# One order changed inside a tick: TensorE's search products first, ScalarE's relu of the search first

## The reference, cut to what matters

```python
# layer 0: two 3x3 convolutions with leaky relu, then a mamba block over L = 4096 tokens
h = exp(d_t * A) * h + (d_t * u_t) * b_t        # scan, 128 channels x 16 states
y = sum_n h * c_t                               # then gate with silu(z) and project
# layer 1
energy_c = xc @ xc.T ; out_c = softmax(energy_c) @ x          # 64 x 64
energy_s = q.T @ k ; attn_s = softmax(energy_s, -1)           # 4096 x 4096
out_s = v @ attn_s.T
out = x + w_bn @ concat(out_c, out_s)
```

## Time and profile before

| | |
|---|---|
| median of 3 runs | 9451.27 us (9447.06 to 9454.93) |
| profiled execution, its own time | 9445.67 us |
| its span, first to last instruction | 9443.9 us |
| mean granted TensorE clock | 0.964 |
| busy share PE, DVE, ACT, POOL | 88%, 79%, 67%, 34% |

### The profile page before, as it was taken

The page is one execution under the profiler, slowest core; times in us unless marked ns, Lnnn a source line. Parts: engine busy times, 40 slices in busy tenths (PEclk is TensorE's granted clock), DMA queues, the critical chain, the costliest instruction groups (busy, mean ns, idle before and its releaser), DMA issues. The chain is left out here.

```text
span 9443.9 us, 135784 instructions
## 1 busy us (share of the span) xinstructions
PE 8334.9 (88%) x38977; PEld 2213.4 (23%) x39622; DVE 7490.6 (79%) x11112; ACT 6298.8 (67%) x12445; POOL 3166.4 (34%) x2315
## 2 busy tenths in 40 slices
PE   7884369998999999998999999998999999989999
PEld 2221112222222222222222222222222222222222
DVE  1114998888898888888898988888898989888832
ACT  1112457777777777777777777777777777777754
POOL 0002543333333333333333333333333333333300
PEclk9997669999999999999999999999999999999999
DMA  5556786766676776766676766766676767667610
GB/s 90 82 85 139 202 204 167 187 171 170 171 178 172 178 183 169 182 173 170 171 181 170 177 174 173 182 173 171 172 178 172 185 171 177 174 166 178 153 27 6
DMA packets 805909, 1511.55 MB, mean 160 GB/s; under 512 B 349800, under 2 KB 383280, under 8 KB 805168
## 3 DMA queue, kind: packets, MB, share of 16 engines
q1 hardware_dynamic: 802096, 1502.63, 65.1%
q10 hardware_dynamic: 3072, 0.40, 0.0%
HBM read 1309.36 MB, written 176.16 MB: 157 GB/s over the span
## 5 line engine op out<-in xcount | busy, mean ns | idle before, releaser
L1208 POOL TENSOR_TENSOR hst<-hst,cbc 128x512 f32<-128x512 f32 x2048 | 2807.6, 1371 | 4892.0 <-ACT carry L965 4289.1
L954 ACT ACTIVATE pr<-bank 128x512 f32<-128x512 f32 x4096 | 2225.7, 597 | 976.4 <-PE bank L836 874.8
L1102 DVE TENSOR_TENSOR_SCAN hst<-dA,carry,bank 128x512 f32<-128x512 f32 x1792 | 2294.0, 1280 | 64.0
L845 PE MATMUL bank<-pr,vt 128*64 128x512 f32 x8192 | 2218.3, 620 | 0.0
L1044 DVE CUSTOM_DVE_ANT_0 gains<-bank,gains 128x512 f32<-128x512 f32 x2048 | 1406.6, 687 | 825.7 <-ACT gains L900 799.6
L1092 DVE TENSOR_TENSOR bank<-lanes,bbc 128x512 f32<-128x512 f32 x2048 | 1707.5, 834 | 79.9 <-DMA lanes<-spread_d 35.2
L782 PE MATMUL bank<-s1kx,s1q 128*128 128x512 bf16 x4096 | 1348.4, 389 | 439.2 <-DVE mxp L1044 398.9
L960 ACT ACTIVATE dA<-lanes,small 128x512 f32<-128x512 f32 x2048 | 1489.2, 727 | 237.4 <-DMA lanes<-spread_d 141.5
L836 PE MATMUL bank<-t2q,t2k 128*128 128x512 bf16 x4096 | 1563.2, 382 | 90.0 <-issue 34.8
L834 PE MATMUL bank<-s1q,s1k 128*128 128x512 bf16 x3451 | 1330.8, 386 | 138.7 <-ACT pr L954 96.9
L900 ACT ACTIVATE gains<-bank 128x512 f32<-128x512 f32 x2048 | 1234.4, 603 | 231.9 <-PE bank L782 226.8
(11 more groups left out here) (110 smaller groups left out, 6369.8 us busy)
## 6 DMA issues: line engine op xcount, KB each, us to landing
lanes<-spread_d SPq DMA_DIRECT2D x2048, 512.0 KB, 5.1
seqt<-seq_d SPq DMA_DIRECT2D x256, 128.0 KB, 4.6
spread_d<-dsp SPq DMA_DIRECT2D x128, 256.0 KB, 2.0
spread_d<-usp SPq DMA_DIRECT2D x128, 256.0 KB, 2.0
bbc<-bc_d SPq DMA_DIRECT2D x128, 256.0 KB, 3.4
cbc<-bc_d SPq DMA_DIRECT2D x128, 256.0 KB, 3.9
xpad<-in_x SPq DMA_DIRECT2D x64, 256.0 KB, 6.4
ypad<-ypad SPq DMA_DIRECT2D x128, 128.0 KB, 2.8
```

The source lines that it names most:

```text
L845: mm = nc.tensor.matmul(ACC[CH * h:CH * (h + 1), :], vt[:, t, :], pr[:, T % PRING, h, :], start=t == 0, stop=t == KT - 1)
L954: nc.scalar.activation(pr[:, T % PRING, h, :], bank_of(("S", T, h))[:], ACT.Exp).then_inc(S["p_full"], 1)
L1102: nc.vector.tensor_tensor_scan(hst[:, T % HRING, :], dA[:, T % 2, :], DBU[:], carry[:, g:g + 1] if sl % CHUNKS else 0.0, ALU.mult, ALU.add ...
L1208: nc.gpsimd.tensor_tensor(h, h, cbc[:, (T - 1) // GROUPS % 2, :], ALU.mult).then_inc(S["hc_in"], 1)
```

## The change

TensorE's tick begins with the search pair; the scores, PV, SUM or Y, and the small products follow. So six bf16 matmuls stand together, and all fp32 products behind them. ScalarE's tick begins with the relu of the search; exp, exp, dA, carry and the rest follow. The ring's order changes with the plan. VectorE's, GpSimd's and SyncE's orders stay as they are, and so does every instruction; only places and the semaphore values that follow from them differ.

```diff
@@ plan
         uses, plan = self.small_uses(T), []
+        near = 2 if self.searches(T) else 0
+        plan += uses[0:near]
         if self.attends(T):
             plan += [("S", T, 0), ("S", T, 1)]
         if self.attends(T - 1):
             plan.append(("PV", T - 1))
-        plan += uses[0:2]
...
-        return plan + uses[2:]
+        return plan + uses[near:]
@@ ScalarE's loop over ticks
                         sl, r = T // GROUPS, T % GROUPS
+                        near = 2 if sched.searches(T) else 0
+                        for e in sched.small_uses(T)[0:near]:
+                            small_use(e)
                         if sched.attends(T):
...
-                        for e in sched.small_uses(T):
+                        for e in sched.small_uses(T)[near:]:
                             small_use(e)
```

## The result

| | before | changed |
|---|---|---|
| median | 9447.06 us (9440.51 to 9454.93, 5 runs) | 9595.04 us (9589.41 to 9598.87, 5 runs) |
| ratio to before | 1 | 1.0157, interval 1.0143 to 1.0171 |
| span of the profiled execution | 9443.9 us | 9596.5 us |
| mean granted TensorE clock | 0.964 | 0.956 |

The change costs 148 us. The forecast was 83 us faster; the time lies in the stated range, on the other side. In the experiments they shift by a few more.

A forecast was written before the change was run, and what follows sets the result against it. Neither VectorE nor TensorE alone bounds; 0.43 us a tick is lost handing over. Relu -1.44, handover +1.3, GpSimd and dt -0.5, times 120 chunks, give -77, with the tail -83: 9368 us; 8 in 10 for 9200 to 9600.

The forecast's parts named there:

- the handover: At r = 10 to 11, scores and PV stand behind max, costing 1.72 us; savings of 0.4 leave net +1.3 per chunk.
- So it is hidden: ScalarE's exp and dA, delayed by max, take 2.6 us from the reduction; the scan wants dA after at least 3.3.
- the pin: max waits for the previous tick's reduction to leave its bank, so scores and PV behind it cannot run ahead.
- The relu at r = 1, -1.44: ScalarE's relu moved first is out before VectorE's tap ends, removing its whole 1.44 us idle per chunk.
- my own rival: Much faster: slack pays for the handover and relu waits vanish everywhere (452 waits, 408 us); about 9170 us, chance 0.15.
- The pair's 0.44: On TensorE, the search pair's distance falls to 0.44 us in all ticks, from 0.53 where narrow fp32 follows.
- GpSimd and VectorE, -0.5 with dt in it: In VectorE's stretch: L1156 -0.85, dt at most +1.0, DBUs and L1150 -0.9 to +2; taken as -0.5 us per chunk.
- The rival on the port: Slower by GpSimd's port: four of nine VectorE-stretch ticks pay 0.67 - 0.12 us each at DBU; 9596 us, chance 0.17.
- The dt wait: The dt product stands 1.97 us later behind the pair; at r = 7 VectorE gets it at most 1.0 us late.
- Slower by the pin: Handover costs 1.5, dt's full 1.0 shows, TensorE can't run ahead: +1.1 per chunk, about 9580 us, chance 0.18.
- Its last part, the clock: Longer single waits might lower TensorE's granted clock once every second chunk, about 1.7 us each, another 100 us.
- the wait at L1139: Sign of being wrong: VectorE waiting over 1 us at L1139, where the late dt product shows.

The follow-up runs named there:

- e5: Changed kernel with only max moved, to directly behind the four score matmuls; dif and the early relu stay: 9370.25 us, 0.9926 of the kernel before.
- e6: e4 plus one added TensorE wait, ahead of the scores, for the reduction of the tick before: 9731.83 us, 1.0306 of the kernel before.
- e11: e5 with ScalarE's order of before, the relu behind carry: 10001.47 us, 1.0583 of the kernel before.
- e7: Kernel before with GpSimd's multiplication by C cut to 16 of 512 columns, leaving out part of the computation: 9124.3 us, 0.9662 of the kernel before.
- e8: Changed kernel with GpSimd's multiplication by C cut to 16 of 512 columns, leaving out part of the computation: 9430.55 us, 0.9987 of the kernel before.
- e3: Changed kernel with small products moved ahead of PV and SUM or Y, except at r = 0: 9580.16 us, 1.0141 of the kernel before.
- e4: Changed kernel with only max moved, behind the scores and PV; dif and relu stay first: 9392.64 us, 0.9943 of the kernel before.
- e10: e5 with ScalarE's carry copy moved ahead of both exps: 9474.98 us, 1.003 of the kernel before.

## Why the prediction was wrong

The step that failed is the handover, priced as **"+1.3"** per chunk for one place, r = 10 to 11. The mechanism was named rightly; its size and its extent were not. TensorE's wait for the reduction in the matmul rows grew from 272.4 us in 1413 ticks to 503.5 us in 1383, that is from 3.1 to 5.8 us in 16 ticks, +2.7, and from three waits in 16 ticks to five (276 and 431 in all). The forecast also had only `max` held, where `dif` is held in 129 of them. Behind it come waits of VectorE that the sum had only for dt: all its waits but the one for the relu rose by 6.0 us in 16 ticks. The sentence on ScalarE, "So it is hidden", held for what it names: the scan waits 22.0 us in 5700 for dA. It is what ScalarE makes of late products that VectorE waits for. e5 and e6 show that the pin decides: moving `max` takes 225 us off, putting its wait back in front of the scores costs 339 us.

- *The relu at r = 1, -1.44.* The direction was right, the term too small: the relu's wait fell from 408 us in 1413 ticks to 60 in 1383, from 4.6 to 0.7 us in 16 ticks. At the very place that was priced it came true and was taken back: in a tick r = 1 of the changed kernel the reduction follows the tap with no wait, but the tap waits 2.27 us for L990, where the earlier trace rows had 0.76.

```profile
8803.78 0.75 DVE L1122 SCALAR_TENSOR_TENSOR cacc<-xin,small,cacc 128x512 f32<-128x512 f32 x1 [2.27 <-ACT cacc L990]
8804.56 0.69 DVE L1048 CUSTOM_DVE_ANT_0 gains<-bank,gains 128x512 f32<-128x512 f32 x1
```

Over the whole stretch this wait rose from 58.1 to 98.7 us; the forecast had let it stay. e11 puts the whole lever at 631 us with e5's order. That the forecast counted one place and the waits showed 452 of them stood in my own rival.
- *The pair's 0.44.* Right: 8781.70 to 8782.15 in the changed kernel's timeline.
- *GpSimd and VectorE, -0.5 with dt in it.* Its two halves must be read apart. L1156 fell from 1258 to 422 ns (-0.84 priced as -0.85), and DBU rose from 824 to 875 ns (+0.8 in 16 ticks), so these two cancel. L1150, which the sum named without a sign, fell from 1132 to 692 ns. Others it did not have: the split behind L1156 (L1161, now L1165) rose from 968 to 1406 ns, and each of the three taps of a chunk fell from 897 to 787. VectorE's work in all fell by 0.6. The rival on the port fell with that, and with e7 and e8; that its number, 9596, is the nearest of all is luck. The Trainium skill (SBUF — State Buffer, Who interferes with whom) calls the port pair that VectorE shares with GpSimd an exclusive lock. The stretched means agree with it. The dt wait was bounded by 1.0 and measured 124.0 / 87 = 1.4 us.
- *Left out.* res, en, turn, PV's copy and Y at its reader L1088: 61 + 69 + 39 + 39 + 31 = 239 us of VectorE's waits in 5700, against 17 before, and 66 us more before the scan. I had moved every small product by 1.97 us and followed only dt. In e3, though, removing such a wait gave 15 us back while the pin stood, and others came in its place.
- *The rivals.* "Slower by the pin" gave 9580 and the kernel took 9595. Its cause is the shown one; that the number agrees is partly luck, since the terms inside were each too small, in both signs. Its last part, the clock, does not carry the loss: the granted clock is 0.956 after and 0.964 before, but e5, with 0.957, is 225 us faster than the changed kernel, and e6, with 0.959, is 137 us slower. What the step from 0.964 costs by itself no run shows.
- *The signs.* The wait for the relu (60 us), L1156 (422 ns), DBU's mean (875) and the pair's distance (0.44) came as listed. Of the listed signs of being wrong one came, the wait at L1139 (now L1143) over 1 us; the granted clock in the stretch fell from 0.99 to 0.98, just to its bound.
- *The whole.* In 16 ticks the relu's relief was 3.9 us, VectorE's other waits rose by 6.0 and its work fell by 0.6: +1.4, or about 170 us for 120 chunks, where 148 were measured. The forecast had -1.44 for the first, and +1.3 with at most 1.0 for dt for the second. A difference of two terms that were each taken at well under half of their size could not carry a sign.

## What to carry to other kernels

When engines meet through a ring of buffers, look for the one instruction of a tick whose buffer the slowest engine frees last, and count what stands behind it in the same queue: work that does not need that engine, and that others wait for, belongs ahead of it. Not all such work is worth it: PV ahead of `max` (e4) was 22 us slower than PV behind it (e5). Moving both halves of a pair because one half is wanted early is the error here; `dif` early and `max` behind the scores gives the gain without the added pin. A wait in a profile that a reordering removes says where lateness shows, and only an experiment says whether time comes back: e3 took 109 us of waiting at one line away and got 15 us.

## What was not expected of the hardware

What VectorE loses to GpSimd moves with the order: L1156 takes 1258 ns before, 422 ns in the changed kernel and 943 ns in e10, with the same operands. In a handover of the changed kernel (r = 11) the granted clock fell to 0.83 over 10 us, as in the earlier trace rows, with the score matmuls at the distance of 1.2 GHz:

```profile
8770.00:8780.00 10.00, 7.40 (x27) 2.01 (x29) 9.57 (x14) 6.17 (x13) 3.79 (x3) 0.83 0.59 165
```

```profile
8776.70 1.03 PE L783 MATMUL bank<-s1kx,s1q 128*128 128x512 bf16 x2 [2.18 <-DVE mxp L1048]
8777.52 0.63 PE L835 MATMUL bank<-s1q,s1k 128*128 128x512 bf16 x1
8777.95 0.63 PE L837 MATMUL bank<-t2q,t2k 128*128 128x512 bf16 x1
...
8779.37 1.41 PE L846 MATMUL bank<-pr,vt 128*64 128x512 f32 x4
```

They stand 0.43 us apart in place of 0.22 after a wait of 2.18 us. TensorE had also stood 2.27 us before 8753.48 and 1.95 us before 8770.42, and there the scores followed at 0.22.
